# Two PSUM banks for the values, a fourth place for transposed probabilities, and DVE's group sums after the last key item

## What is computed

```python
def _L0_xattn_ref(hidden_states, context, attention_mask, q_w, q_b, k_w, k_b, v_w, v_b):
    q = _split_heads(hidden_states @ q_w.T + q_b)
    k = _split_heads(context @ k_w.T + k_b)
    v = _split_heads(context @ v_w.T + v_b)
    scores = jnp.einsum('bhqd,bhkd->bhqk', q, k) / jnp.sqrt(jnp.float32(HD))
    scores = jnp.where(mask, -jnp.inf, scores)
    probs = jax.nn.softmax(scores, axis=-1)
    ctx = jnp.einsum('bhqk,bhkd->bhqd', probs, v)

x = x + _L0_xattn_ref(_layernorm(x, axis=-1), ctx_1024, mask_BxS2_ik0, ...)
x = x + _L0_attn_ref(_layernorm(x, axis=-1), L0_attn_W_q)
x = x + _L0_ffn_ref(_layernorm(x, axis=-1), L0_ffn_gate_w, ...)
```

## Time and profile before

| | |
|---|---|
| runs | 1257.81, 1259.71, 1259.81 us, median 1259.71 |
| the profiled execution, its own time | 1257.15 us |
| its span, first to last instruction | 1255.3 us |
| mean granted clock of PE | 0.997 |
| PE matmuls | busy 1216.4 us, 97% |
| PE weight loads (PEld) | busy 1121.1 us, 89% |
| DVE | busy 881.1 us, 70% |
| ACT | busy 700.3 us, 56% |
| POOL | busy 147.2 us, 12% |

### The profile page before, as it was taken

How to read it: one execution, slowest core, us unless ns; L and a number is a source line. 1 busy time by engine, 2 the same in 40 slices (tenths; PEclk the granted TensorE clock), 3 DMA queues, 4 the chain that set the end, 5 groups by cost and what they waited for, 6 DMA issues and landing times.

```text
span 1255.3 us, 25775 instructions
## 1 busy us (share of the span) xinstructions
PE 1216.4 (97%) x10197; PEld 1121.1 (89%) x10197; DVE 881.1 (70%) x2309; ACT 700.3 (56%) x1266; POOL 147.2 (12%) x84
## 2 busy tenths in 40 slices
PE   7999999999999999999999999999889999999998
PEld 7999999999999999999999899998768888989986
DVE  6566667566666656666665666677779888777887
ACT  6456445645644564564456356445555676767663
POOL 0003101300400150040013004000012000000012
PEclk9999999999999999999999999999999999999999
DMA  8002200310220031022003102200316777767663
GB/s 300 33 1 90 82 1 2 109 63 1 90 82 1 2 117 55 1 90 83 1 4 120 50 1 90 96 1 2 112 68 209 269 251 253 248 230 260 238 217 132
DMA packets 61062, 127.20 MB, mean 101 GB/s; under 512 B 3645, under 2 KB 21193, under 8 KB 60825
## 3 DMA queue, kind: packets, MB, share of 16 engines
q1 hardware_dynamic: 58776, 118.97, 27.5%
q0 software_dynamic: 2176, 6.72, 1.6%
HBM read 120.01 MB, written 14.32 MB: 107 GB/s over the span
## 4 chain that ended last, share of the span: by engine, by line
PE 70%; DVE 19%; ACT 7%; issue 2%; DMA 1%; SPq 0%; ACTq 0%; DVEq 0%
PE work L921 16%; PE ptp L921 14%; PE ptp_pv L921 8%; PE work L1311 6%; PE ptp_pv L1094 5%; PE work L959 4%; PE work L1313 3%; DVE pt L1593 3%; DVE kk_lo L1474 2%; PE ptp L1334 2%; PE ptp L1337 2%; PE ptp L1335 2%; PE ptp L1336 2%; PE ptp L1338 2%; DVE folded L1601 2%
## 5 line engine op out<-in xcount | busy, mean ns | idle before, releaser
L585 POOL TENSOR_TENSOR cx_lo<-raw,cx_hi 128x1664 fp32r<-128x1664 f32 x28 | 106.2, 3792 | 672.2 <-ACT cx_hi L646 672.2
L921 PE MATMUL work<-cx_hi,kw_hi 128*128 128x400 f32 (+1 forms) x504 | 175.3, 348 | 0.7 <-DVE cx_lo L1495 0.7
L921 PE MATMUL work<-cx_hi,kw_lo 128*128 128x400 f32 (+1 forms) x504 | 173.5, 344 | 0.0
L921 PE MATMUL work<-cx_lo,kw_hi 128*128 128x400 f32 (+1 forms) x504 | 173.2, 344 | 0.0
L921 PE MATMUL ptp<-vw_hi,cx_hi 128*128 128x256 f32 x576 | 167.8, 291 | 0.0
L921 PE MATMUL ptp<-vw_lo,cx_hi 128*128 128x256 f32 x576 | 162.9, 283 | 0.0
L921 PE MATMUL ptp<-vw_hi,cx_lo 128*128 128x256 f32 x576 | 162.9, 283 | 0.0
L659 ACT ACTIVATE kk_hi<-work,biasT 128x400 fp32r<-128x400 f32 (+1 forms) x128 | 75.4, 596 | 135.2 <-PE work L921 132.5
L1094 PE MATMUL ptp_pv<-pt,vv 64*128 64x256 f32 x1664 | 141.9, 296 | 8.0 <-DVE pt L1593 3.9
L1311 PE MATMUL work<-xg,w_hi 128*128 128x352 f32 x512 | 142.7, 354 | 2.1 <-DVE xg L1763 1.0
L1474 DVE SCALAR_TENSOR_TENSOR kk_lo<-work,biasT,kk_hi 128x400 fp32r<-128x400 f32 (+1 forms) x128 | 78.8, 632 | 92.3 <-ACT kk_hi L659 91.6
(11 more groups left out here) (293 smaller groups left out, 2783.7 us busy)
## 6 DMA issues: line engine op xcount, KB each, us to landing
w1raw<-in_w SPq DMA_DIRECT2D x32, 1024.0 KB, 5.1
w2raw<-in_w SPq DMA_DIRECT2D x32, 1024.0 KB, 6.5
raw<-in_ctxT SPq DMA_DIRECT2D x31, 832.0 KB, 5.1
pr<-in_mask SPq DMA_DIRECT2D x8, 800.5 KB, 4.3
xrow<-x_rows SPq DMA_DIRECT2D x7, 256.0 KB, 5.8
y_rows<-y_out_rows POOLq DMA_DIRECT2D x7, 256.0 KB, 2.4
xs<-in_x SPq DMA_DIRECT2D x1, 1024.0 KB, 9.3
qwraw<-in_qwT SPq DMA_DIRECT2D x1, 1024.0 KB, 6.9
```

Source lines behind the costliest of these rows:

```text
L585: pool.tensor_tensor(cx[1][:, :, sl], raw[:, k % 2], cx[0][:, :, sl].bitcast(F32), ALU.subtract).then_inc(c_lo, 1)
L921: last = pe.matmul(dst, lhs(i, c), rhs(j, c), start=(c == 0 and (i, j) == (0, 0)), stop=(c == n - 1 and (i, j) == (1, 0)))
```

## The change

Value items alternate between `ptp[0]` and `ptp[1]`, and each waits for the drain of the item two before it; T0 has no wait for a value item any more. The probabilities get a fourth place, `pt_late`, in SBUF rows of `hn`, or in the last batch `pt_end` in rows of `raw`; ACT's wait becomes W(j-4). In the even group T4 is issued after W1 and no longer after W0, and T5 and T6 both after W2. DVE's `group_out` loses its last five instructions to a new function `group_rows`. For the even group that is called after the key item k7 (after `q` in the last half); for the odd group it follows `group_out` as before.

```diff
--- before.py
+++ after.py
@@ -98,7 +98,7 @@
 FIRST_K = 2 * NKC
 FIRST_C, REST_C = slice(0, C // 2), slice(C // 2, C)
 NPT = 2 * (KT + 1)
-PTD = 3
+PTD = 4
 TPH = KT // 2 + 1
 
 
@@ -124,7 +124,7 @@
 
 TURNED_BY = [2, TPH + 2, 2 * TPH]
 FIRST_TURNS = [(2, 3), (TPH + 2, TPH + 3)]
-NEXT_TURN = {0: 4, 2: 5, 3: 6, 4: 7, 5: 8, 8: 11, 9: 12, 10: 13}
+NEXT_TURNS = {1: (4,), 2: (5, 6), 4: (7,), 5: (8,), 8: (11,), 9: (12,), 10: (13,)}
 PAIR_OF = [3, 3, 2, 0, 1, 2, 0, 1, 2, 1, 2, 0, 1, 2]
 
 
@@ -190,7 +190,7 @@
 
 def bank_of(last, step):
 
-    return step[2] % PTD if spare(step) else BANKS[last][RING[last].index(step)]
+    return step[2] % 2 if spare(step) else BANKS[last][RING[last].index(step)]
 
 
 def before_bank(b, last, step):
@@ -245,6 +245,8 @@
         rsum = sb(top, "rsum", [P, B, 8], F32)
         rtok = sb(top, "rtok", [P, TT, 16], F32)
         xs = sb(top, "xs", [P, TT, D], F32)
+        with ExitStack() as m2:
+            pt_late = sb(m2, "pt_late", [P, 2, 2, 2, P], F32R)
         hn = sb(top, "hn", [P, TT, D], F32)
 
 
@@ -255,6 +257,9 @@
             kk = [sb(m, f"kk_{n}", [P, 2, LKP], F32R) for n in ("hi", "lo")]
             pr = sb(m, "pr", [P, 4, KP], F32)
             negmask = sb(m, "negmask", [P, LKP], BF16)
+            with ExitStack() as m2:
+                sb(m2, "self_weight_space", [P, C, D], F32)
+                pt_end = sb(m2, "pt_end", [P, 2, 2, 2, P], F32R)
             raw = sb(m, "raw", [P, 2, C, CC], F32)
             qbd = [sb(m, f"qbd_{n}", [P, 2, P], F32R) for n in ("hi", "lo")]
             folded = sb(m, "folded", [P, 2, 2 * P], F32)
@@ -262,7 +267,7 @@
             nmx = sb(m, "nmx", [P, 8], F32)
             with ExitStack() as m2:
                 vv = sb(m2, "vv", [P, KT, 2, 2, 2, 2 * HD], F32R)
-                pt = sb(m2, "pt", [P, PTD, 2, 2, 2, P], F32R)
+                pt = sb(m2, "pt", [P, PTD - 1, 2, 2, 2, P], F32R)
 
             qw_hi = sb(m, "qw_hi", [P, C, D], F32R)
             xnT = [sb(m, f"xnT_{n}", [P, C, T], F32R) for n in ("hi", "lo")]
@@ -421,9 +426,13 @@
             start = 2 * P if jj == 1 else 0
             return pairs[PAIR_OF[jj]][:, :, start:start + units * S].rearrange("p a (u q) -> p a u q", q=S)
 
-        def pt_part(j, n, part):
-
-            return pt[:, j % PTD, 0:n, :, part, :].rearrange("p n r (a q) -> p a (n r) q", a=2)
+        def place_of(last, j):
+
+            return pt[:, j % PTD] if j % PTD < PTD - 1 else (pt_end if last else pt_late)
+
+        def pt_part(last, j, n, part):
+
+            return place_of(last, j)[:, 0:n, :, part, :].rearrange("p n r (a q) -> p a (n r) q", a=2)
 
         def scattered(ph, e):
 
@@ -724,12 +733,12 @@
                 total = rsum[:, b, r:r + 1] if isinstance(b, int) else rsum[:, bass.ds(b, 1), r]
                 act.activation(row, row, ACT.Exp, bias=nmx[:, r:r + 1], accum_out=total).then_inc(exp_done, 1)
 
-            def pt_item(b, j):
+            def pt_item(b, last, j):
 
                 act.wait_ge(pt_full, NPT * b + j + (2 if j % (2 * TPH) == 0 else 1))
                 act.wait_ge(pt_used, NPT * b + pt_before(j))
                 n = min(2, KT - 2 * (j % TPH))
-                copy(pt_part(j, n, 0), turned_block(j, 2 * n), pt_hi)
+                copy(pt_part(last, j, n, 0), turned_block(j, 2 * n), pt_hi)
 
             def fold(b, g):
 
@@ -753,7 +762,7 @@
                     if kind == "e":
                         exponentials(b, a)
                     for j in turns(step):
-                        pt_item(b, j)
+                        pt_item(b, last, j)
                     if kind == "w":
                         fold(b, a)
                     if kind == "l":
@@ -987,10 +996,8 @@
                     return
                 if not spare(step):
                     pe.wait_ge(w_free, before_bank(b, last, step))
-                elif k >= PTD:
-                    pe.wait_ge(w_free, count(b, last, ("v", a, k - PTD)))
-                elif k == PTD - 1:
-                    pe.wait_ge(pv_free, 4 * b + 2 * a + 1)
+                elif k >= 2:
+                    pe.wait_ge(w_free, count(b, last, ("v", a, k - 2)))
                 if kind == "k":
                     key_item(b + 1 if a == 0 else b, a, k, bank)
                 elif kind == "v":
@@ -1055,7 +1062,6 @@
                 g, jj, first = j // TPH, j % (2 * TPH), 2 * (j % TPH)
                 h, pair = g // 2, PAIR_OF[jj]
                 if jj == 0:
-                    pe.wait_ge(w_free, count(b, last, ("v", h, 5)))
                     pe.wait_ge(pv_free, 4 * b + 2 * h + 1)
                 if jj == 2:
                     pe.wait_ge(w_free, count(b, last, ("v", h, TPH - 1)))
@@ -1078,7 +1084,7 @@
                                            ident[rows, rows])
                 ins.then_inc(pt_full, 1)
 
-            def weigh(b, j):
+            def weigh(b, last, j):
 
                 g, first = j // TPH, 2 * (j % TPH)
                 pe.wait_ge(pt_lo, NPT * b + j + 1 + PTD)
@@ -1093,7 +1099,7 @@
                             rows = slice(S * a, S * (a + 1))
                             ins = pe.matmul(sums[a][:, rt * 2 * P:(rt + 1) * 2 * P],
                                             vv[rows, kt, g % 2, rt].rearrange("p a d -> p (a d)"),
-                                            pt[rows, j % PTD, n, rt].rearrange("p a d -> p (a d)"),
+                                            place_of(last, j)[rows, n, rt].rearrange("p a d -> p (a d)"),
                                             start=(kt == 0 and rt == 0), stop=(kt == KT - 1 and rt == 1))
                 ins.then_inc(pt_used, 1)
 
@@ -1102,9 +1108,9 @@
                 for jj in FIRST_TURNS[g % 2]:
                     turn(b, last, base + jj)
                 for jj in range(TPH * (g % 2), TPH * (g % 2 + 1)):
-                    weigh(b, base + jj)
-                    if jj in NEXT_TURN:
-                        turn(b, last, base + NEXT_TURN[jj])
+                    weigh(b, last, base + jj)
+                    for later in NEXT_TURNS.get(jj, ()):
+                        turn(b, last, base + later)
 
             def body(b, last=False):
                 for step in STEPS[last]:
@@ -1586,11 +1592,11 @@
                         dve.tensor_scalar(nmx[:, a:a + 1], nmx[:, a:a + 1], 1024.0, 1 / 1024.0,
                                           ALU.mult, ALU.mult).then_inc(nmx_done, 1)
 
-            def pt_item(b, j):
+            def pt_item(b, last, j):
 
                 dve.wait_ge(pt_hi, NPT * b + j + (2 if j % (2 * TPH) == 0 else 1))
                 n = min(2, KT - 2 * (j % TPH))
-                dve.tensor_tensor(pt_part(j, n, 1), turned_block(j, 2 * n), pt_part(j, n, 0).bitcast(F32),
+                dve.tensor_tensor(pt_part(last, j, n, 1), turned_block(j, 2 * n), pt_part(last, j, n, 0).bitcast(F32),
                                   ALU.subtract).then_inc(pt_lo, 1)
 
             def group_out(b, g):
@@ -1600,6 +1606,9 @@
                     dve.tensor_tensor(folded[rows, 0], sums[1][rows, cols], folded[rows, 0], ALU.add)
                     ins = dve.tensor_tensor(folded[rows, 1], sums[1][others, cols], folded[rows, 1], ALU.add)
                 ins.then_inc(pv_free, 1)
+
+            def group_rows(b, g):
+
                 dve.wait_ge(pv_free, 4 * b + g + 2)
                 dve.tensor_tensor(summed, folded[:, 0], folded[:, 1], ALU.add).then_inc(sums_done, 1)
                 dve.wait_ge(sums_done, 4 * b + g + 1)
@@ -1614,9 +1623,11 @@
                 for step in STEPS[last]:
                     kind, a, j = step
                     for i in turns(step):
-                        pt_item(b, i)
+                        pt_item(b, last, i)
                     if kind == "w":
                         group_out(b, a)
+                    if kind == "w" and a % 2:
+                        group_rows(b, a)
                     if last and step == ("v", 0, 1):
                         row_weights(range(EARLY))
                     if kind == "r":
@@ -1631,6 +1642,8 @@
                         row_weights(range(EARLY, TT))
                     if kind in "vskanq":
                         item(b, last, step)
+                    if kind == "q" or step == ("k", a, 2 * NKC - 1):
+                        group_rows(b, 0 if step == ("k", 1, 2 * NKC - 1) else 2)
 
                     if step == ("s", 3, NKC - 1):
                         query_blocks(b, 1)
```

## The result

The changed kernel takes 1264.49 us (median of 6 runs, 1263.66 to 1265.45) where the kernel before takes 1259.76 (6 runs, 1256.37 to 1260.00). The ratio is 1.0043, with a 95% interval of 1.0031 to 1.0056: slower by 0.4%.

A forecast was written before the change was run, and what follows sets the result against it. PE, busy 97% of the span, was taken as the bound, so DVE and ACT count only where PE waits. -4.4 - 4.0 + 17.2 = +8.8 us on 1257.15 gives 1266.0, 1268.5 at the median; forecast 1268 us, range 1262 to 1274.

The forecast's parts named there:

- T0's term: Ahead of T0, at each half's start: without its wait for v5, T0 starts 0.3 us sooner, -4.4 us in 15 halves.
- the step to the median: 2.6 us added to the forecast because the median shown, 1259.71, lay above the profiled execution: 1266.0 becomes 1268.5.
- The sums behind k7: DVE between the groups: sums after k7's drain hold item 9, so W9 starts 1.15 us later; +17.2 us in 15 halves.
- The walk: DVE from k6's drain to item 9: idle 1.05 us, k7's drain, sums, then item 9 2.19 us after W7.
- T4 later and four places: Even group: T4 no longer waits, W2 waits for item 2, T5's item sets W5; 0.27 us less a half, -4.0 us.
- The bound of 0.57: Upper bound on T0's gain per half: the whole wait of its weight load, 9.1 / 16.
- Two banks for the values: Value items: v2's new wait for v0's drain has 0.14 us margin, so nothing lost; 2 us kept in the range.
- a new wait outside the three places: Sign against the forecast: if any half showed a new wait outside the places treated, the sum would be wrong.
- 15 halves and not 16: T0's gain is counted in 15 halves, because in the last half T2 follows soon and DVE sets it.
- The covered sums: Rival: DVE's 1.4 us of sums find room ahead of W9, leaving only the two gains, 1251.3 us; chance 6%.
- the change does less than it says: Rival: T0's other waits or v2's drain take the gain's place, +15.2, so 1275 us; chance 7%.
- The clock: Rival: the clock falls in PE's new hole of some 1.6 us in each of 15 halves, 1294 us; chance 4%.

The follow-up runs named there:

- e2: The kernel before with only the even group's five SBUF sums moved behind k7: 1275.38 us, ratio 1.0138 to before.
- e5: The changed kernel with the even group's five SBUF sums between k6's and k7's drain: 1248.55 us, ratio 0.9920 to before.
- e6: e1 with the five SBUF sums of every group moved from DVE to POOL: 1242.59 us, ratio 0.9872 to before.
- e4: The kernel before with only the fourth place and the later T4 and T6: 1254.43 us, ratio 0.9974 to before.
- e3: The kernel before with only the value items put on two banks: 1252.21 us, ratio 0.9953 to before.
- e7: e1 with T12 issued ahead of W9 instead of behind it: 1242.86 us, ratio 0.9880 to before.
- e10: e8 with T5 issued ahead of W2 instead of behind it: 1230.86 us, ratio 0.9786 to before.
- e9: The changed kernel run once more without edit, beside the kernel before on the same chip: 1264.77 us against 1258.03, ratio 1.0051.
- e1: The changed kernel with the even group's five SBUF sums back directly behind group_out: 1247.51 us, ratio 0.9918 to before.
- e8: The edits of e6 and e7 together, no other edit: 1234.11 us, ratio 0.9817 to before.

## Why the prediction was right

The forecast was slower, 1268 us in a range of 1262 to 1274; measured were 1264.5 and 1264.8. The direction, the mechanism and each place are as forecast, and the 3.5 us to the middle have two causes of about the same size, T0's term and the step to the median. Both made the forecast too slow. T0's gain was 6.6 us by the profile and not 4.4; smaller misses of the other terms give 0.7 of that back, and the step to the median is the remaining 2.0.

- **The sums behind k7, forecast +1.15 us a half.** Measured +1.13 in the profile, and e2 gives 17.3 us for the part alone against 17.2. The walk held in each step: an idle DVE of 1.06 (1.05), the sums from k7's drain on, item 9 right behind them (2.16 us after W7, forecast 2.19, and 1.04 before). Its reason is shown by e5 and e6: 1.15 is the sums' 1.40 us less the 0.25 that they cost already.
- **T4 later and four places, forecast -0.27 a half.** Measured -0.24, and 3.6 us for the part alone (e4) against 4.0. W2 waits for item 2, T5's item sets W5, as said.
- **T0 without its wait, forecast -0.3 a half.** This term was sized too small: -0.44 in the profile and 5.8 us in e3 against 4.4. The step at fault is "where a transpose follows other matmuls and waits for nothing, the same distance is 0.28". That row has a transpose behind key matmuls of 128 rows. Ahead of T0 stand score matmuls of 64 rows, and T0 is of 64 rows too; between two such the distance is 0.18 to 0.19, as it is between one group of score matmuls and the next. The other way round the trace has the longer distance too: 0.27 from score matmuls to a value item's, which has 128 rows. The remaining 0.05 is that T0 and T1 themselves take 0.59 instead of 0.64 us, which the prediction did not count; why is not shown. The bound of 0.57 held it.
- **Two banks for the values, forecast nothing.** The time between the groups did not change (42.24 us a half in e3). v2 does wait for v0's drain in 7 halves now, a new wait outside the three places, which the prediction had named as a sign of a wrong sum. But it is a wait of the weight load alone, and v2's first matmul follows the scores by 0.27 us as before:

```profile
PEld ptp L930 <- DVE vv L1569: 1.8, 7, 0.3
```

- **15 halves and not 16.** In the last half T0 comes sooner as well, but T2 then waits 1.4 us for v6's drain where it waited 0.9, and from T0 to T2 it is 4.7 us instead of 4.3. The gain of T0 is lost again there, as the prediction's count had it.
- **The step from the profiled execution to the median.** The sum's +8.8 was set against 1257.15 and then 2.6 us were added, because the median shown lay so far above. That was scatter of the kernel before: in 35 further runs its medians were 1258.03 to 1258.25, and the changed kernel's profiled execution (1264.53) lies at its own median. Without the 2.6 the forecast would have been 1266.0.
- **The rivals.** The covered sums are out: W9 follows item 9 by 0.05 us before and after. That the change does less than it says is out too: T0 and the even group gained. The clock did not fall in the new holes; it stayed at its upper level from 15 us to 922 us of the span. The window over one of the holes shows the full clock, as the nearest case before did:

```profile
533.00:537.00 4.00, 2.54 (x50) 2.41 (x48) 3.72 (x9) 1.83 (x5) 0.00 (x0) 1.00 0.00 0
```

## What to carry to other kernels

Work that fills an engine's wait costs little (0.25 us of 1.40 here), and moving it "out of the way" behind the wait makes it cost its whole length: ask of the queue what the engine does while the next operand is made, not only who waits for the moved work. Where a transpose and the weighing ahead of it wait for the same signal, issue the transpose first; its item's way through ACT and DVE (1.83 us here) then runs beside the weighing (e7, e10). Take the price of a switch between two kinds of matmul from a row with the same two kinds. And compare profiles over the stretch that the change touches, where the medians also carry the scatter of the rest.

## What the runs showed of the hardware

In the last half of the attention the clock does not always hold its upper level, and it falls at different times in different executions, those of one kernel too. Both profiles of the changed kernel have an idle time of PE of 1.53 us in the last odd group, from 911.74 us in the first and from 911.84 us in e9. In the first the granted clock reads 1.00 from 910 to 918 us; in e9 it reads 0.79 there and 0.50, the lower level of 1.2 GHz, from 913 to 916 us. The last odd group takes 7.76 us in the first and 8.65 in e9. In e4 the lower level lasted longer:

```profile
901.00:909.00 8.00, 6.92 (x59) 6.17 (x60) 3.96 (x8) 2.76 (x7) 0.00 (x0) 0.57 0.51 186
```

In that stretch the matmuls of the last odd group start 0.21 us apart instead of 0.11 to 0.12, and the group takes 9.4 us, where it took 7.8 in the profile before the change, with the clock at 1.00. The profiles of e1, e3, e5, e7 and e10 show the lower clock at still other times of the last half; e8's shows it nowhere between 14 and 1227 us. The 15 holes of 1.5 us in the changed kernel, each with dense matmuls on both sides, left the clock at its upper level throughout. In the last half, with shorter work around them, an idle time of 1.8 us (e4) was followed by the lower level, and in e3 so were two of 1.1 and 0.7 us shortly one after the other; the same 1.8 us before the change, and the same pair in the changed kernel (its first profile), were not.

This goes with part of the scatter of the kernel before. Of its 35 later runs 13 have a mean granted clock of 0.996 and a median of 1259.17 us, 19 have 0.997 and 1257.52, and 3 have 0.998 and 1256.65. That is a relation in the record and not an experiment: no run held the clock fixed.
